# One transformer layer on one core: the second group's experts moved into the first pass, weighted values in bursts of a row, some weight splits on GpSimd

## The chip, the cores and the metric

The kernel runs on one core of a Trainium2 chip. The metric is the time of the device in microseconds. The kernel before took 824.49 us (median of 3 runs, 824.25 to 825.43); its profiled execution took 822.76 us, with a span of 821.0 us between the first and the last instruction.

## The reference, cut to what matters

The input x is 32 rows of 128 tokens of width 128. For all tokens:

```python
# 1. routed experts (8 of width 64, top 2) and a shared one of width 128
y = sum_over_experts(route_weight * (leaky(x @ w_gate) * (x @ w_up)) @ w_down)
y = y + (leaky(x @ sw_gate) * (x @ sw_up)) @ sw_down
# 2. banded attention of one head on y (span 32), layer norm, added to x
# 3. layer norm, then attention of 16 heads of width 64 with one shared key and value,
#    a null key, normed queries and keys, a position bias and a softmax over 129 keys
# 4. layer norm, then a feed-forward net 128 -> 2 x 512 (gated) -> 512 -> 512 -> 128,
#    added to the result of 2
```

All in float32. The kernel gets that precision for most projections from three matmuls with a weight and an input that are each split into a high part and a low part (`three`, L1199).

## The kernel before, in words

The 32 rows are worked on in 8 groups of 4 rows (512 tokens). A group goes through stage A (experts `rw`, `exp`, `down`; banded attention `qkv`, `scores`, `mix`; norms `ln1`, `ln2`; projections `xnT`, `kv`, `q`, and the sums `qs`, `qst`, `kT`), stage B (the attention of 16 heads: `sim`, `max`, `ex`, `inv`, `pn`, `PT`, `PV`, `z`) and stage C (feed-forward: `zT`, `l1` to `l4`). The stages are a software pipeline: a pass holds stage A of one group, stage B of the one before it and stage C of the one before that. The first pass ("fill") holds A of group 0 and the setting up, the second ("start") A of group 1 and B of group 0, then come five "steady" passes, "seventh", "last" and "drain".

Within a pass each engine follows a list written out by hand, `ORDER` (L53 to L192), one list for each engine and kind of pass; `passes` (L238) turns it into calls. Engines wait for each other by counting semaphores, and each engine is strictly in order: what waits blocks all behind it in its list. Step names in the lists have a number: `exp.0` to `exp.4` are five chunks of 128 hidden units (two groups of three matmuls, gate and up, and for `exp.0` to `exp.3` one matmul that spreads the routing weights), `sim.0` to `sim.11` three bursts of heads for each of four rows, `PT.0` to `PT.15` the transposes of four heads each, `PV.0` to `PV.7` the weighted values of eight heads each.

The PSUM banks come in rings: M of three, S of two (`sim`, `qs`), T of two (`PT`, `PV`). `bank_plan` (L251) gives banks in the order of TensorE's list, and `free` (L1205) makes TensorE wait until the last user of a bank has been drained. In the fill pass stage A uses a ring F of four banks (M and one of T).

What matters around the change:

- `experts_low` (`wl`, L828) and `part_low` (`pl`, L909) take the low parts of the weights on VectorE; `pl.0` to `pl.3` stand in the fill pass, `pl.4` and `pl.5` (h1 and h2, 2048 elements a partition each) in the start pass. Both h1 and h2 are loaded into `hA`, one after the other: `load_square` (`hw`, L515) waits for the split of h1 before it loads h2.
- The experts of a group: TensorE `expert` (L1225), ScalarE `expert` (L682) leaky gate out of PSUM, VectorE `expert` (L945) two products out of PSUM. `gs` and `hT` hold the results and are used again by stage A.
- SyncE's list: `load_x` (L519) loads the group's x in both layouts, after the table of the position bias has been written to memory and read back (L506 to L510). `flip_bias` (`fl`, L1192) on TensorE needs that read.
- GpSimd: `q_norm` (`qn`, L614) is a power of 16 columns for a row, `bias` (L619) adds the mask to the position bias for four heads, `p_norm` (`pn`, L631) multiplies four heads' exponentials by the inverse sums. `score` (`sim` on VectorE, L1078) waits for `qn` of its row, for `bias` of its heads and for the transposes that last read `sm`.
- `pv` on TensorE (L1332): for eight heads two matmuls, one into each half of the partitions, into one bank of T; ScalarE's `ot_copy` (L743) takes them out.
- `warm` (L1175) are matmuls whose results nobody reads; they stand in the fill pass alone.

## Time and profile before

| | us |
|---|---|
| median of 3 runs | 824.49 |
| profiled execution | 822.76 |
| its span | 821.0 |
| fill pass, to the first `sim.0` | 0 to 71.8 |
| start pass, to the next `sim.0` | 71.8 to 141.8 |
| a steady pass (five) | 94.7 to 95.1 |
| seventh, last, drain | 87.2, 94.1, 24.0 |

The passes are told apart by the matmuls of L1321 with number 0. Over the span TensorE has matmuls in flight for 786.9 us (96%), ScalarE is busy for 606.6 us, VectorE for 584.7 us and GpSimd for 448.9 us. A matmul's row shows how long it was in flight, and the next one starts before it ends, so starts are to be compared rather than durations. "Idle before" is the time that an engine stood still ahead of a row, and behind it stands what ended the wait.

### The profile page before, as it was taken

Reading aid. Unit: us, or ns where it says so; the run is one execution under the profiler, and the core shown is the slowest. Engines: PE = TensorE matmul, PEld = TensorE weight load, DVE = VectorE, ACT = ScalarE, POOL = GpSimd, SP = SyncE. Lnnn points to the kernel's source line nnn. Section 1 sums busy time; section 2 is a strip of 40 time slices with the busy share of each in tenths; the row PEclk is TensorE's granted clock in tenths of the full one; section 3 lists DMA queues with packets and bytes.
Section 4 is the critical chain, followed back from the end, with each engine's and each line's share of the span. In section 5 each row is a group of like instructions: output and inputs, shape, how many; then the busy total and the mean of one; then the engine's idle time right before and its main releaser. Section 6 shows DMA issues by size and latency. Waiting matters only on the chain.

```text
span 821.0 us, 16705 instructions
## 1 busy us (share of the span) xinstructions
PE 786.9 (96%) x5368; PEld 595.9 (73%) x5368; DVE 584.7 (71%) x1581; ACT 606.6 (74%) x1652; POOL 448.9 (55%) x388
## 2 busy tenths in 40 slices
...
DMA packets 15589, 16.99 MB, mean 21 GB/s; under 512 B 1408, under 2 KB 13072, under 8 KB 15120
## 3 DMA queue, kind: packets, MB, share of 16 engines
...
q10 hardware_dynamic: 304, 0.01, 0.0%
...
## 4 chain that ended last, share of the span: by engine, by line
PE 54%; ACT 19%; DVE 8%; issue 7%; POOL 5%; DVEq 0%; ACTq 0%; POOLq 0%
PE ps_M L1202 25%; ACT sb_sm L733 8%; PE ps_S L1321 5%; PE ps_z L1349 4%; PE ps_T L1336 4%; PE ps_T L1329 4%; PE ps_M L1248 4%; ACT L733 3%; PE ps_M L1381 3%; DVE sb_sm L1089 2%; ACT sb_al L774 2%; ACT L774 2%; PE ps_S L1303 2%; POOL sb_rq L617 2%; ACT sb_pT L740 2%
## 5 line engine op out<-in xcount | busy, mean ns | idle before, releaser
L733 ACT ACTIVATE sb_sm<-sb_sm,sb_nmx 128x129 f32<-128x129 f32 x512 | 199.2, 392 | 33.3 <-DVE sb_nmx L1097 32.8
L634 POOL TENSOR_TENSOR sb_sm<-sb_sm,sb_rden 128x512 f32<-128x512 f32 x128 | 135.8, 1064 | 144.9 <-DVE sb_rden L1102 144.9
L627 POOL TENSOR_TENSOR sb_biasm<-sb_bias,sb_maskn 128x512 f32<-128x512 f32 x128 | 170.9, 1343 | 79.0 <-DVE sb_sm L1089 55.0
L1089 DVE SCALAR_TENSOR_TENSOR sb_sm<-ps_S,sb_rq,sb_biasm 128x129 f32<-128x129 f32 x512 | 140.5, 342 | 55.9 <-PE ps_T L1329 43.2
L617 POOL TENSOR_TENSOR sb_rq<-sb_qss,sb_mhalf 128x16 f32<-128x16 f32 x32 | 92.1, 2903 | 27.4 <-DVE sb_qss L1074 27.4
L1321 PEld LDWEIGHTS ps_S<-sb_k,sb_qs 64*128 64x128 f32 x1024 | 65.1, 187 | 43.6 <-issue 43.1
L733 ACT ACTIVATION_READ_ACCUMULATOR sb_sm<-sb_sm,sb_nmx 128x1 f32 x512 | 96.6, 189 | 0.0
L740 ACT ACTIVATE sb_pT<-ps_T 128x512 f32<-128x512 f32 x128 | 74.4, 588 | 22.3 <-PE ps_T L1329 22.2
L1321 PE MATMUL ps_S<-sb_k,sb_qs 64*128 64x129 f32 x1024 | 83.0, 291 | 4.4 <-DVE sb_sm L1089 3.5
L1097 DVE TENSOR_REDUCE sb_nmx<-sb_sm 128x4 f32<-128x516 f32 x128 | 85.5, 675 | 0.4
L1329 PE MATMUL ps_T<-sb_ident,sb_sm 128*128 128x128 f32 x512 | 76.5, 276 | 3.6 <-POOL sb_sm L634 3.2
L1329 PEld LDWEIGHTS ps_T<-sb_ident,sb_sm 128*128 128x128 f32 x512 | 59.2, 141 | 17.1 <-issue 5.2
L1336 PE MATMUL ps_T<-sb_pT,sb_vs 128*64 128x512 f32 x256 | 66.4, 612 | 3.0 <-ACT sb_pT L740 3.0
L1349 PE MATMUL ps_z<-sb_wout,sb_oT 128*128 128x128 f32 x512 | 67.5, 279 | 0.4 <-ACT sb_oT L747 0.4
L1349 PEld LDWEIGHTS ps_z<-sb_wout,sb_oT 128*128 128x128 f32 x512 | 62.2, 192 | 5.2 <-ACT sb_oT L747 1.4
L1049 DVE TENSOR_SCALAR sb_qs<-ps_M,sb_cols 128x512 f32<-128x512 f32 x62 | 45.6, 744 | 16.9 <-ACT sb_gs L721 6.5
L1202 PE MATMUL ps_M<-sb_hBh,sb_h2h 128*128 128x512 f32 (+1 forms) x144 | 55.6, 386 | 0.8 <-DVE sb_hBl L923 0.8
L1202 PE MATMUL ps_M<-sb_hAh,sb_h1h 128*128 128x512 f32 (+1 forms) x144 | 55.0, 382 | 0.5 <-DVE sb_hAl L923 0.5
L1202 PE MATMUL ps_M<-sb_hAh,sb_h1l 128*128 128x512 f32 (+1 forms) x144 | 53.1, 369 | 0.0
L1202 PE MATMUL ps_M<-sb_hBl,sb_h2h 128*128 128x512 f32 (+1 forms) x144 | 53.1, 369 | 0.0
L1202 PE MATMUL ps_M<-sb_hBh,sb_h2l 128*128 128x512 f32 (+1 forms) x144 | 53.1, 369 | 0.0
L1202 PE MATMUL ps_M<-sb_hAl,sb_h1h 128*128 128x512 f32 (+1 forms) x144 | 53.1, 369 | 0.0
...
## 6 DMA issues: line engine op xcount, KB each, us to landing
...
sb_hA<-in_h SPq DMA_DIRECT2D x2, 1024.0 KB, 6.7
...
sb_sm<-toeplitz SPq DMA_DIRECT2D x1, 1024.0 KB, 5.8
...
```

Of the source, the lines that this page charges most:

```text
L617: pool.tensor_tensor(rq[:, cut], qss[:, cut], mhalf[:], ALU.pow).then_inc(q_rnorm.sem, 1)
L627: pool.tensor_tensor(biasm[:, heads, 1:NK], bias0[:, heads], maskn[:, j // 4].unsqueeze(1).broadcast_to([128, 4, S]), ALU.add)\
L634: pool.tensor_tensor(sm[:, heads, 1:NK], sm[:, heads, 1:NK], rden[:, heads].unsqueeze(2).broadcast_to([128, 4, S]), ALU.mult)\
L733: ins = act.activation(sm[:, h], sm[:, h], ACT.Exp, bias=nmx[:, h:h + 1], accum_out=den[:, h:h + 1])
L740: act.activation(pT[:, heads].rearrange("p h s -> p (h s)"), bank(g, "PT", j)[:], ACT.Copy)\
L1089: ins = dve.scalar_tensor_tensor(sm[:, h], bank(g, "sim", n, odd)[:, m * NK:(m + 1) * NK], rq[:, k * HEADS + h:k * HEADS + h + 1], biasm[: ...
L1097: dve.tensor_reduce(nmx[:, heads], sm[:, heads], AX, ALU.max, negate=True).then_inc(max_ready.sem, 1)
L1202: ins = pe.matmul(ps, w[i], x[j], start=start and n == 0, stop=stop and n == 2)
L1321: ins = pe.matmul(ps[odd][:, m * NK:(m + 1) * NK], qs[half, lo + m, k * S:(k + 1) * S], k2[half, k], start=True, stop=True)
L1329: ins = pe.transpose(ps[:, h * S:(h + 1) * S], sm[:, j % 4 * 4 + h, 1:NK], ident[:])
L1336: ins = pe.matmul(ps[DH * odd:DH * (odd + 1)].rearrange("p (h s) -> p h s", h=4), vs[:, n // 2], pT[:, n % 2 * 8 + odd:n % 2 * 8 + 8:2], s ...
L1349: ins = pe.matmul(zbank[:, k * D:(k + 1) * D], oT[:, c], wout[:, c], start=(c == 0), stop=(c == NP - 1))
```

## The change

- `pv` is called four times a group instead of eight; each call does the sixteen heads of a row in eight instructions, into both banks of T, and waits for all four `PT` copies of the row. ScalarE's copies stay eight.
- Stage N: `rwn`, `expn`, `xhn`, `xln` in the fill pass are `rw`, `exp`, `xh`, `xl` of group 1. Their steps are gone from the start pass. Group 1's gate tiles are in `x1`, its hidden tiles in `hA` and `res`; its x is loaded directly after the split of group 0's, ahead of the position table. The load of h1 (`hw.0`) moves to the start pass, behind group 1's `down`; h2's stays behind h1's split.
- `wl` and `pl.0` to `pl.3` are done by GpSimd, `wl` in two instructions of 640 columns; `pl.4` and `pl.5` stay on VectorE.
- All lists are written anew.

```diff
     "pe fill": """
-        lg.0 warm.0 pb.0 warm.1-5 pb.1 warm.6 lg.1-2 warm.7 rw.0 exp.0 lg.3-4 exp.1 lg.5 exp.2 lg.6 pb.2 lg.7
-        exp.3 warm.8 exp.4 down.0 warm.9 pb.3 warm.10 qkv.0 scores.0 mix.0 warm.11-13 fl.0-2 warm.14 fl.3 xnT.0
-        warm.15-16 q.0-2 kv.0 q.3 qs.0-2 q.4-7 qs.3-7 warm.17 qst.0 kT.0 warm.18-21
+        lg.0 warm.0 pb.0 warm.1-4 pb.1 warm.5 lg.1-2 warm.6-7 lg.3 rw.0 exp.0 lg.4 pb.2 lg.5 exp.1 lg.6-7 exp.2
+        warm.8 pb.3 warm.9 exp.3-4 down.0 warm.10 fl.0 warm.11 qkv.0 scores.0 warm.12 rwn.0 mix.0 expn.0 fl.1
+        warm.13-16 expn.1 warm.17 fl.2-3 expn.2 xnT.0 expn.3 q.0-1 kv.0 q.2-4 qs.0-3 q.5-7 qs.4-7 qst.0 warm.18
+        expn.4 warm.19-20 kT.0 warm.21
     "pe start": """
-        sim.0 rw.0 sim.1 exp.0-1 sim.2 exp.2 sim.3 exp.3 PT.0-1 exp.4 PV.0 sim.4 PT.2 down.0 PT.3 sim.5 PT.4
...
+        sim.0-1 down.0 sim.2 PT.0-1 sim.3 PT.2 sim.4 qkv.0 PT.3 scores.0 sim.5 PV.0 mix.0 PT.4-5 sim.6-7 z.0
...
     "act start": """
...
+        ex.0-2 down.0 PT.0 ex.3 PT.1-2 qkv.0 ex.4 PT.3 ex.5 PV.0-1 ex.6-7 ph.4 PT.4-7 ex.8 PV.2 ex.9-10 PV.3
+        PT.8 xnT.0 ex.11 PT.9-10 q.0 ex.12 PT.11 ph.5 ex.13 PV.4 q.1 PV.5 q.2-3 ex.14 q.4 ex.15 PT.12-13 q.5-7
     "dve fill": """
...
+        xl.0 cg.0 rt.0 pb.0 nk.0 pb.1 rt.1-4 pb.2 x0.0 rw.0 pb.3 nk.1 exp.0-1 rt.5-6 exp.2-3 rt.7 exp.4 rt.8
+        down.0 xln.0 rt.9 qkv.0 rwn.0 scores.0 maskn.0 mix.0 expn.0 ln1.0 expn.1 ln2.0 expn.2 xnT.0 expn.3 q.0-1
+        kv.0 q.2-4 kT.0 q.5 ssq.0 ssc.0 expn.4 q.6 vs.0 q.7
     "dve start": """
...
+        sim.0 max.0 sim.1 max.1 inv.0-1 max.2 sim.2 inv.2 max.3 sim.3 down.0 sim.4 inv.3 max.4-5 qkv.0 inv.4
+        scores.0 inv.5 sim.5 max.6-7 mix.0 inv.6 sim.6 inv.7 ln1.0 max.8 sim.7 max.9 ln2.0 inv.8 max.10 sim.8
+        inv.9 pl.4 inv.10 max.11 xnT.0 sim.9 inv.11 max.12 sim.10 maskn.0 max.13 q.0 sim.11 kv.0 inv.12-13 q.1
+        max.14-15 q.2-3 inv.14 kT.0 q.4 inv.15 q.5-6 ssq.0 pl.5 ssc.0 q.7 vs.0
     "pool fill": """
-        pb.0-1 nb.0 nk.0 xb.0 ln1.0 ln2.0 bias+.0-2 kv.0 bias+.3 qn.0-3
+        pb.0 nb.0 wl.0 pb.1 xb.0 pl.0 nk.0 ln1.0 ln2.0 pl.1-2 bias+.0-2 kv.0 bias+.3 pl.3 qn.0-3
     "pool start": """
...
+        bias.4 pn.0-1 bias.5 pn.2 bias.6-8 pn.3 bias.9 xb.0 pn.4-5 bias.10-11 ln1.0 bias.12 pn.6-7 ln2.0 pn.8-9
     "sp start": """
-        rw.0 hw.1 maskn.0
+        own.0 hw.0 maskn.0 hw.1
...
-            def pv(g, n):
+            def pv(g, k):
-                ps = free(g, "PV", n, 0, (v_shifted, 1), (pt_copied, 2 * n + 2))
-                for odd in range(2):
...
+                for n in (2 * k, 2 * k + 1):
+                    ps = free(g, "PV", k, n % 2, (v_shifted, 1), (pt_copied, 4 * k + 4))
+                    for odd in range(2):
...
+            def experts_low(g, k):
+                pool.wait_ge(w_high, 1)
+                for n in range(2):
+                    pool.tensor_tensor(wgu[1][:, n], wgu_raw[:, n], wgu[0][:, n].bitcast(fp32), ALU.subtract).then_inc(w_low, 1)
+
+            def part_low(g, k):
+                name = PARTS[k]
+                pool.wait_ge(parts_high[name], 1)
+                pool.tensor_tensor(parts[name][1][:], raw[name], parts[name][0][:].bitcast(fp32), ALU.subtract)\
+                    .then_inc(parts_low[name], 1)
...
             def load_square(g, k):
-                sp.wait_ge(*((routed, 2 * ROUTE_OPS), (parts_low["h1"], 1))[k])
+                sp.wait_ge(*((y_psum.sem, y_psum.at(1, 1)), (parts_low["h1"], 1))[k])
```

In the steady list of TensorE the twelve `sim` bursts, the chunks and the layers are the same steps as before in another order; `PV` stands in four places there (five runs of `PV` before), and the runs of 512 column matmuls of L1202 are 20 instead of 16. In the seventh list `PV` has 4 runs instead of 8, in the last and the start list 4 instead of 7.

## Rows read from the trace of the kernel before

**Rows 1.** Windows by pass: busy us (instructions) of PE, PEld, DVE, ACT, POOL; clock, DMA.
```profile
0.00:71.80 71.80, 56.63 (x361) 44.48 (x361) 50.16 (x145) 24.46 (x41) 20.56 (x45) 0.98 0.37 129
71.80:141.80 70.00, 63.98 (x484) 45.10 (x483) 61.56 (x163) 53.05 (x174) 54.56 (x41) 1.00 0.08 26
331.60:426.30 94.70, 93.90 (x638) 70.71 (x637) 69.11 (x186) 73.29 (x201) 54.06 (x45) 1.00 0.05 10
615.70:702.90 87.20, 86.19 (x587) 62.54 (x587) 65.80 (x181) 70.74 (x198) 56.69 (x46) 1.00 0.01 1
702.90:797.00 94.10, 91.16 (x623) 72.74 (x620) 54.47 (x154) 80.38 (x212) 45.49 (x38) 1.00 0.02 7
```

**Rows 2.** Windows, two stretches of the start pass, same columns.
```profile
69.97:87.00 17.03, 15.52 (x109) 11.83 (x110) 15.38 (x40) 12.26 (x36) 17.03 (x10) 1.00 0.00 1
87.00:141.80 54.80, 50.28 (x393) 34.98 (x393) 48.01 (x127) 41.99 (x141) 39.36 (x32) 1.00 0.10 33
```

**Rows 3.** Timeline, head of the start pass: start, us, engine, what.
```profile
69.97 8.64 POOL L617 TENSOR_TENSOR sb_rq<-sb_qss,sb_mhalf 128x16 f32<-128x16 f32 x3 [2.50 <-DVE sb_qss L1074]
...
82.68 2.04 POOL L634 TENSOR_TENSOR sb_sm<-sb_sm,sb_rden 128x512 f32<-128x512 f32 x2
...
86.11 1.64 DVE L1089 SCALAR_TENSOR_TENSOR sb_sm<-ps_S,sb_rq,sb_biasm 128x129 f32<-128x129 f32 x6
```

**Rows 4.** Lines of the expert step: count, ns minimum/median/maximum, first and last start.
```profile
L687 ACT ACTIVATE sb_gs<-ps_M x39: 572/597/602, 21.9 to 627.4; 128x512 f32<-128x512 f32 x39
L958 DVE TENSOR_TENSOR sb_hT<-ps_M,sb_gs x31: 690/692/694, 26.8 to 626.5; 128x512 f32<-128x512 f32 x31
```

**Rows 5.** Timeline, expert matmuls of a steady pass.
```profile
332.44 0.50 PE L1202 MATMUL ps_M<-sb_xh,sb_wguh 128*128 128x512 f32 x1
332.78 0.39 PE L1202 MATMUL ps_M<-sb_xl,sb_wguh 128*128 128x512 f32 x1
333.01 0.40 PE L1202 MATMUL ps_M<-sb_xh,sb_wgul 128*128 128x512 f32 x1
```

**Rows 6.** Timeline, fill pass: splits, position table, first qkv.
```profile
12.23 1.49 DVE L830 TENSOR_TENSOR sb_wgul<-sb_hT,sb_wguh 128x1280 fp32r<-128x1280 f32 x1
...
40.72 0.47 PE L1202 MATMUL ps_M<-sb_yTh,sb_wqkvh 128*128 128x512 f32 x1 [0.66 <-issue]
...
42.97 0.34 ACT L670 ACTIVATE sb_pT<-ps_S,sb_pb 16x128 f32<-16x128 f32 x1
...
50.68 4.34 PE L1196 MATMUL ps_S<-sb_sm,sb_pT 128*128 128x512 f32 x6 [2.80 <-DMA sb_sm<-toeplitz]
...
59.32 1.22 DVE L912 TENSOR_TENSOR sb_w12l<-sb_al,sb_w12h 128x1024 fp32r<-128x1024 f32 x1
```

**Rows 7.** Timeline, a GpSimd addition, then VectorE and GpSimd side by side.
```profile
95.46 1.29 POOL L607 TENSOR_TENSOR sb_xs<-sb_xs,sb_rows 128x512 f32<-128x512 f32 x1
...
108.15 1.61 DVE L1017 TENSOR_TENSOR sb_hT<-sb_hT,sb_rows 128x512 f32<-128x512 f32 x1
...
132.71 2.65 DVE L912 TENSOR_TENSOR sb_h2l<-sb_hA,sb_h2h 128x2048 fp32r<-128x2048 f32 x1
...
133.16 3.10 POOL L634 TENSOR_TENSOR sb_sm<-sb_sm,sb_rden 128x512 f32<-128x512 f32 x1
...
136.31 0.66 PE L1329 MATMUL ps_T<-sb_ident,sb_sm 128*128 128x128 f32 x4 [2.00 <-POOL sb_sm L634]
```

**Rows 8.** The page's DMA issues, loads of h1 and h2.
```profile
sb_hA<-in_h SPq DMA_DIRECT2D x2, 1024.0 KB, 6.7
```

**Rows 9.** Timeline, PV in a steady pass: two calls in a row, and one alone.
```profile
360.28 1.94 PE L1336 MATMUL ps_T<-sb_pT,sb_vs 128*64 128x512 f32 x8
...
362.27 0.72 PE L1321 MATMUL ps_S<-sb_k,sb_qs 64*128 64x129 f32 x8
...
386.84 1.08 PE L1336 MATMUL ps_T<-sb_pT,sb_vs 128*64 128x512 f32 x4 [0.61 <-ACT sb_pT L740]
387.85 0.94 PE L1321 MATMUL ps_S<-sb_k,sb_qs 64*128 64x129 f32 x12
```

More of the change, by code:

```diff
@@ L67 @@
[L67 to L69 removed]
+        sim.0 rw.0 exp.0-1 sim.1 exp.2-3 sim.2 exp.4 down.0 sim.3 zT.0 PT.0-1 qkv.0 l1.0-1 PT.2 l1.2 scores.0
+        PT.3 l1.3 sim.4 PV.0 sim.5 l2.0 PT.4 l2.1 z.0 sim.6 PT.5 l2.2 z.1 l2.3 PT.6 mix.0 PT.7 sim.7 l3.0 sim.8
@@ L118 @@
-        exp.4 rt.8 down.0 rt.9 qkv.0 scores.0 mix.0 pl.1 ln1.0 pl.2 ln2.0 xnT.0 maskn.0 pl.3 q.0-2 kv.0 q.3-5
-        kT.0 ssq.0 ssc.0 q.6-7 xl.0 vs.0
+        xl.0 cg.0 rt.0 pb.0 nk.0 pb.1 rt.1-4 pb.2 x0.0 rw.0 pb.3 nk.1 exp.0-1 rt.5-6 exp.2-3 rt.7 exp.4 rt.8
+        down.0 xln.0 rt.9 qkv.0 rwn.0 scores.0 maskn.0 mix.0 expn.0 ln1.0 expn.1 ln2.0 expn.2 xnT.0 expn.3 q.0-1
+        kv.0 q.2-4 kT.0 q.5 ssq.0 ssc.0 expn.4 q.6 vs.0 q.7
     """,
     "dve start": """
-        xl.0 rw.0 sim.0 max.0 sim.1 exp.0 max.1 exp.1 sim.2 inv.0 max.2 inv.1 exp.2 max.3 inv.2 exp.3 sim.3
@@ L123 @@
-        inv.3 max.4 sim.4 inv.4 max.5 exp.4 max.6 inv.5 down.0 sim.5 inv.6 max.7 pl.4 qkv.0 scores.0 sim.6 inv.7
-        max.8 mix.0 sim.7 inv.8 max.9 ln1.0 sim.8 inv.9 max.10-11 ln2.0 inv.10 sim.9 xnT.0 max.12 inv.11 sim.10
-        inv.12 max.13-14 q.0 kv.0 sim.11 q.1 maskn.0 inv.13 q.2-3 max.15 q.4 inv.14 kT.0 inv.15 q.5 pl.5 ssq.0
-        q.6 ssc.0 q.7 vs.0
+        sim.0 max.0 sim.1 max.1 inv.0-1 max.2 sim.2 inv.2 max.3 sim.3 down.0 sim.4 inv.3 max.4-5 qkv.0 inv.4
+        scores.0 inv.5 sim.5 max.6-7 mix.0 inv.6 sim.6 inv.7 ln1.0 max.8 sim.7 max.9 ln2.0 inv.8 max.10 sim.8
@@ L132 @@
-        max.11 ln2.0 inv.9-11 sim.9 xnT.0 max.12 kv.0 maskn.0 sim.10 q.0 inv.12 max.13 q.1 max.14 q.2 inv.13
-        sim.11 l4.0 max.15 inv.14 kT.0 q.3-5 inv.15 ssq.0 q.6 ssc.0 q.7 vs.0
+        xl.0 rw.0 ln3.0 sim.0 exp.0-1 sim.1 exp.2 max.0 exp.3 max.1 inv.0 exp.4 max.2 sim.2 zT.0 max.3 inv.1-2
+        down.0 zl.0 sim.3 max.4 inv.3 qkv.0 l1.0-1 h1.0-1 l1.2-3 sim.4 scores.0 max.5 h1.2 inv.4 h1.3 max.6
+        sim.5 max.7 inv.5-6 h2.0 inv.7 sim.6 max.8 h2.1-2 mix.0 h2.3 sim.7 max.9 inv.8 sim.8 max.10-11 inv.9
@@ L134 @@
+        ln1.0 ln2.0 inv.10-11 xnT.0 sim.9 kv.0 sim.10 max.12 inv.12 max.13-14 q.0 inv.13 kT.0 q.1 inv.14 l4.0
+        q.2 sim.11 max.15 maskn.0 q.3 inv.15 q.4 ssq.0 q.5-6 ssc.0 vs.0 q.7
     """,
     "dve seventh": """
-        rw.0 xl.0 ln3.0 exp.0 sim.0 exp.1-2 sim.1 max.0 exp.3-4 inv.0 max.1-2 zT.0 inv.1 sim.2 max.3 down.0
-        inv.2 zl.0 inv.3 sim.3 qkv.0 l1.0-1 h1.0 max.4 l1.2 h1.1 sim.4 h1.2 max.5 l1.3 max.6 scores.0 h1.3 inv.4
-        sim.5 inv.5 max.7 inv.6 sim.6 inv.7 max.8 mix.0 sim.7 inv.8 max.9-10 ln1.0 sim.8 max.11 inv.9 h2.0 ln2.0
```

179 lines of the change are left out of this document (95 added, 84 removed).

## The prediction

> **What bounds the kernel now.** I read the windows by pass first. In a steady pass TensorE has work in flight for 93.9 of 94.7 us while VectorE has 69 and ScalarE 73 [rows 1]: there, and in the seventh pass, the order of TensorE's own list is the time, and other engines count only where they make it stand. In the start pass it is otherwise: TensorE 64, VectorE 61.6, GpSimd 54.6 of 70.0 us, and in the fill pass nobody is full (56.6 and 50.2 of 71.8), which is a chain of latencies. So the work that the change takes out of the start pass is worth what that pass's own bounds allow, and I read those in two stretches.
>
> Head of the start pass: from 69.97 us, when the inverse norms of group 0 begin, to 87.0 us GpSimd is busy 17.03 of 17.03 us [rows 2]. It does four powers of 2.9 us (three of them are the 8.64 us row), one bias, two normalisations (2.04 us) and a bias, and then VectorE can start the fourth burst of scores at 86.11 us [rows 3]: 86.11 - 69.97 = 16.1 us that GpSimd sets alone. Rest of the start pass: 54.8 us with VectorE busy 48.0 and TensorE 50.3 [rows 2]: VectorE with its waits.
>
> **The change part by part.** My clock is the profiled execution (822.76 us, 1.7 us below the median of the runs); I take differences from it and put them on the median, 824.5.
>
> *Experts of group 1, out of the start pass.* Removed from it: on TensorE 4 x 7 + 6 = 34 matmuls of 0.23 us (332.78 to 333.01 us [rows 5]), 7.9 us; on VectorE 9 products of 0.69 us [rows 4], 6.2 us, and the split of x, 0.7; on ScalarE 5 gates of 0.6 us [rows 4] and two copies, 4.2 us. Almost all of VectorE's part (exp.0 to exp.3, eight products) stands before 86.11 us, that is inside the 16.1 us of GpSimd, whose list at that point is the same steps as before. There it buys nothing unless VectorE then does later work early, and the new list of VectorE has down.0 only behind sim.3. So of 6.2 us I count only exp.4, 0.6 us (results start 0.6 us apart), and on TensorE the four routing transposes, 0.5 us, now behind the next sim.0. The bounds are 0 and TensorE's 7.9 us.
>
> *VectorE's split of h2 (pl.5).* It now stands between ssq and ssc, beside TensorE's PV.3 of 2 us. Before, it ran at 132.71 us beside the last normalisation, which took 3.10 us against a usual 1.04, and TensorE stood 2.00 us for it [rows 7]. I count -2.2 us with the restart. What is late next: h2's load can only be issued behind pl.4, which has moved from the row of the fifth maximum to behind inv.9; the load takes 6.7 us [rows 8], and ph.5 stands in ScalarE's list four ScalarE steps of about 6 us later, with the exponentials ex.13 and all of group 1's remaining squares queued behind it. I price that wait at +0.9 us (0 to 4).
>
> *Start pass, smaller things.* PV in 4 runs and not 7 (below), -0.4 us; four entries fewer into 512 column runs at 0.1 us (0.34 against 0.23 us to the next start [rows 5]), -0.4. Sum of the start pass: -0.6 - 0.5 - 2.2 + 0.9 - 0.8 = -3.2 us (-10 to +2).
>
> *Fill pass.* Added on its way: 34 expert matmuls, 9 products and 5 gates, 0.7 us of split, and the routing transposes. Taken off VectorE: wl 1.49 us, and the splits pl.0 to pl.3, of which w12 has 1.22 us for 1024 columns [rows 6]. The new products stand one pair (1.3 us) in each place where VectorE waited for a power on GpSimd or for a transpose, and the 8 us of matmuls where TensorE did warming up; VectorE has 71.8 - 50.2 = 21.6 us free there [rows 1]. So most of it is hidden. What isn't, by my walk through the lists: TensorE does lg.3 and an extra warm ahead of exp.0 (about +0.8 us on its start at 20.7); fl.0 and a warm stand ahead of qkv.0, which began at 40.72 us. fl.0 needs the position table, which landed 7.7 us behind the copy at 42.97 us [rows 6]. In the new lists that copy stands before exp.3, at about 33 us by my walk, so the table is there at about 41, just when the low part of y is. The rest of the chain keeps its lengths. On GpSimd the splits cost, by the nearest row, an addition of two tiles, 1.29 us for 512 columns [rows 7]: wl 3.2 us, wq2 and w12 2.6 us each; the other end is VectorE's price, half of that. wl can start when its high part is there (about 16 us) and ends at 19, before TensorE is at exp.0; wq2 ends about 1 us before q.0 wants it; w12 lies between the last bias of row 0 and the first power, where GpSimd waited 2.50 us [rows 3]. If that cover were gone they would cost 2.6 us at most at the last place. I take +1.5 us for the fill pass (-1 to +5).
>
> A rule bears on this. Where GpSimd and VectorE both work on tiles in SBUF the rows show stretched instructions: an addition of VectorE took 1.61 us beside GpSimd, and one of GpSimd 3.10 us beside VectorE's split [rows 7]. The Trainium skill, SBUF — State Buffer, section "Who interferes with whom", says that a VectorE instruction with two SBUF inputs and a GpSimd instruction that reads SBUF exclude each other for the whole instruction, whichever comes first. By that rule each split on GpSimd (3 us for wl) can stop VectorE's routing chain of small two-input steps for its own length, up to some 3 us at the start of the fill pass; by the rows the stretch is the other's remaining time, which is the same thing, and TensorE's logits cover it here. It goes into the upper end for the fill pass alone.
>
> *PV in one burst.* Two calls in a row took 362.27 - 360.28 = 1.99 us, one alone 387.85 - 386.84 = 1.01 us and about 0.1 of entry [rows 9]: a merge gives 0.1 to 0.15 us, no more. One steady run of PV stood 0.61 us for ScalarE's copy of the transposes between two calls [rows 9]; in the new list a layer and two bursts of scores stand in that place, so it goes. Steady pass: -0.6 - 0.14, and four more entries into 512 column runs at up to 0.1 us, +0.25: -0.5 us, five times, -2.5 us (a pass -2 to +1.2, since the order is new and its stalls can't be read from the old trace). Seventh: four merges, -0.5; last: three, -0.4 and -0.3 for its waits, ScalarE having 80 of 94 us [rows 1]: -1.2 us together. The drain list is the same but for two swaps: 0.
>
> Sum: -3.2 + 1.5 - 2.5 - 1.2 = -5.4 us; 824.5 - 5.4 = 819.1, told as 819 us.
>
> **The rivals.**
> *The moved experts are worth their full TensorE time.* The start pass would shrink by 7.9 us and the fill pass hide all: 824.5 - 7.9 - 0.5 (start's other gains less the wait for h2) - 3.2 = 813 us. For it: TensorE's 7.9 us and VectorE's 6.2 lie in the passes where VectorE has 61.6 of 70 us [rows 1]. Against it: GpSimd's 17.03 of 17.03 us at the head [rows 2].
> *The fill pass gets longer.* One mechanism: fl.0 stands in front of qkv.0, so if the position table lands later than y's low part all of stage A of group 0 waits for it. Each microsecond of lateness is one of the total. The total turns slower when the table lands more than 5.4 us later than I reckon, at 46.5 us; it landed at 50.6 before [rows 6]. If the copy ahead of it came at 42 us again and not at 33: +8.5 us, 827.5 us. Against it: ScalarE's new list has that copy in front of two expert chunks.
> *What one pass gives the next takes.* The fill pass takes +4, the start pass gives -3.2, the steady order gives nothing: 824.3 us, no change. For it: the steady passes have few stalls to give.
> That merged PV does not do what it says is not a rival of its own; it is worth under 2 us in all.
>
> **How the numbers follow.** Forecast 0.47 (its own range 815 to 823), full worth 0.27, no change 0.12, longer fill (or another new stall of this size) 0.14. What can be told from no change is 0.2%, 1.6 us. Of the forecast's case 0.02 falls inside the 0.2%, and the no-change case spills a little to both sides: faster 0.73, same 0.12, slower 0.15. Range: the full-worth case gives the low end with the steady passes at -1 us each, 811; the high end takes in no change and the beginning of the longer fill, 826.
>
> **What would show it.** The first sim.0 at 73.3 us (71.8 before); the first power of GpSimd 1.5 us later and the fourth score burst again 16.1 us behind it; start to steady at about 140 us instead of 141.8; ph.5 with a wait for a DMA; steady passes of 94.2 us; no wait of PV for L740 in them. Wrong if: the score burst comes sooner than 16 us behind the first power, or a new wait of over 1 us appears in every steady pass.

## The result, and the profile after

The changed kernel takes 829.50 us (median of 8 runs, 826.82 to 834.75) against 824.37 us of the kernel before in the same session (8 runs, 822.18 to 826.25): ratio 1.0071, 95% interval 1.0056 to 1.0085. It is slower by about 5.9 us; 819 us was forecast (811 to 826), faster. The profiled execution took 826.82 us, the shortest of the eight, its span 824.9 us; that of before has a span of 821.0 us, so the two traces differ by 3.9 us, and the table below accounts for these 3.9.

I cut both traces where TensorE turns the sums of the query squares of the next group (before: 69.4, 139.3, ... 613.3, 700.2 us). Windows of the changed kernel by pass (fill, start, third steady, seventh), then the start pass of the kernel before between the same two cuts; columns as in [rows 1]:

```profile
0.00:75.10 75.10, 60.59 (x370) 48.45 (x370) 59.23 (x145) 26.80 (x45) 26.16 (x50) 0.98 0.31 109
75.10:144.50 69.40, 59.01 (x452) 42.32 (x453) 52.76 (x150) 50.26 (x168) 55.46 (x41) 0.95 0.13 41
334.90:429.70 94.80, 93.80 (x637) 70.89 (x635) 67.81 (x185) 72.72 (x201) 54.67 (x44) 1.00 0.04 10
619.30:703.60 84.30, 83.38 (x574) 62.42 (x572) 67.35 (x183) 69.75 (x197) 54.93 (x44) 1.00 0.00 1
```
```profile
69.40:139.30 69.90, 63.88 (x485) 45.06 (x483) 61.60 (x160) 53.05 (x174) 54.59 (x40) 1.00 0.08 26
```

| stretch | before | after | difference | forecast |
|---|---|---|---|---|
| fill pass | 69.4 | 75.1 | +5.7 | +1.5 |
| start pass | 70.0 | 69.4 | -0.6 | -3.2 |
| five steady passes | 474.0 | 474.8 | +0.8 | -2.5 |
| seventh | 86.9 | 84.3 | -2.6 | with the next: -1.2 |
| last and drain | 120.8 | 121.3 | +0.5 | |

The forecast cut the passes elsewhere, at the first `sim.0`, so its column doesn't fit these rows exactly. By its own cut the changed kernel has the first `sim.0` at 80.4 us (71.8 before, 73.3 forecast) and the next one at 146.5 us (141.8 before, about 140 forecast):

```profile
80.43 0.94 PE L1351 MATMUL ps_S<-sb_k,sb_qs 64*128 64x129 f32 x12 [0.49 <-ACT sb_k L756]
```

By that cut the fill pass grew by 8.6 us where +1.5 was forecast, and the start pass shrank by 3.9 us where -3.2 was forecast. The two cuts differ because the first score burst comes 5.3 us behind the turned sums and no longer 2.4: the last expert quarter and the turn of the keys stand between them. GpSimd's powers, and with them the head of the start pass, begin at the turned sums in both kernels, so I keep that cut. By it the start pass lost 5 us of TensorE's busy time and 9 of VectorE's (TensorE's last moved quarter is still inside it), yet it is as long as it was, and the fill pass grew by four times what I had given it. The timeline of the changed kernel there (start, us, engine, what; columns as in [rows 6]), and behind it the norm in the kernel before:

```profile
55.29 0.46 POOL L612 TENSOR_TENSOR sb_wkv2l<-sb_res,sb_wkv2h 128x128 fp32r<-128x128 f32 x1
55.36 5.24 DVE L1031 TENSOR_SCALAR sb_hT<-sb_x,sb_mv,sb_rstd 128x128 f32<-128x128 f32 x4
...
55.70 2.37 POOL L612 TENSOR_TENSOR sb_wq2l<-sb_oT,sb_wq2h 128x1024 fp32r<-128x1024 f32 x1
...
58.04 3.71 POOL L655 TENSOR_TENSOR sb_biasm<-sb_bias,sb_maskn 128x512 f32<-128x512 f32 x3
...
60.66 0.65 PE L1308 MATMUL ps_T<-sb_ident,sb_hT 128*128 128x128 f32 x3 [3.69 <-DVE sb_hT L1031]
```
```profile
55.73 1.11 DVE L1002 TENSOR_SCALAR sb_hT<-sb_x,sb_mv,sb_rstd 128x128 f32<-128x128 f32 x4 [1.19 <-POOL sb_rstd L599]
```

The row to read is VectorE's second layer norm of group 0: four instructions, 5.24 us. In the kernel before the same four took 1.11 us, with GpSimd idle. Here GpSimd runs two low parts and three bias products at the same time, its own rows at their usual length, and TensorE stands 3.69 us for the norm. Behind that wait its clock is low; the timeline of TensorE just after, and the window around it:

```profile
61.74 0.63 PE L1232 MATMUL ps_M<-sb_xl,sb_wguh 128*128 128x512 f32 x1
62.17 0.63 PE L1232 MATMUL ps_M<-sb_xh,sb_wgul 128*128 128x512 f32 x1
```
```profile
61.00:64.50 3.50, 3.50 (x11) 2.83 (x10) 1.97 (x4) 1.28 (x2) 0.75 (x1) 0.52 0.00 0
84.00:90.30 6.30, 6.30 (x14) 2.41 (x11) 3.18 (x10) 4.29 (x22) 6.30 (x5) 0.73 0.00 0
```

Matmuls of 512 columns start 0.43 us apart, where they are 0.23 apart in [rows 5]: granted clock 0.52, the lower of the two levels (1.2 GHz) for all of it. The second window is the down product of the start pass, behind 2 us of TensorE's waiting. A second collision stands at the end of the fill (changed kernel, then the norm of the keys before):

```profile
71.12 3.07 DVE L1091 TENSOR_TENSOR sb_hT<-sb_hT,sb_rk 128x256 f32<-128x256 f32 x2
...
71.34 2.57 POOL L612 TENSOR_TENSOR sb_w12l<-sb_al,sb_w12h 128x1024 fp32r<-128x1024 f32 x1
...
75.11 0.33 PE L1340 MATMUL ps_S<-sb_ident,sb_ssT 128*128 128x128 f32 x1 [1.34 <-DVE sb_ssT L1098]
```
```profile
67.26 0.83 DVE L1061 TENSOR_TENSOR sb_hT<-sb_hT,sb_rk 128x256 f32<-128x256 f32 x2
```

The norm of the keys took 0.83 us before and takes 3.07, beside the low part of w12. The query copy and the sums stand behind it on VectorE. Adding up: 4.1 us of the first collision, 1.4 of the slow clock behind it (seven matmuls 0.20 us later each) and 2.2 of the second are 7.7; the pass grew by 5.7, so some of it was hidden. What was hidden can be told from the stretch that holds both collisions, from the first matmul of qkv to the turned sums: 28.6 us before (40.72 to 69.36), 34.0 in the changed kernel (41.09 to 75.11).

### The profile page after: what moved, and what is told of

The parts are those of the page before. It is cut to its first block, busy times and chain, and to the rows that moved or that the text cites. A ratio compares the mean times of both kernels' runs of the same rounds, so it can differ in the third digit from the quotient of the medians.

```text
span 824.9 us, 16692 instructions
## 1 busy us (share of the span) xinstructions
PE 786.3 (95%) x5368; PEld 601.0 (73%) x5368; DVE 579.7 (70%) x1576; ACT 601.5 (73%) x1650; POOL 459.5 (56%) x394
## 4 chain that ended last, share of the span: by engine, by line
PE 72%; DVE 10%; POOL 6%; issue 5%; ACT 5%; DMA 0%; DVEq 0%; ACTq 0%; POOLq 0%
PE ps_M L1232 38%; PE ps_S L1351 7%; PE ps_T L1359 5%; PE ps_z L1380 5%; PE ps_T L1367 5%; PE ps_M L1278 3%; DVE sb_sm L1119 3%; POOL sb_rq L645 3%; ACT sb_sm L762 2%; POOL sb_biasm L655 2%; POOL sb_sm L662 2%; PE ps_S L1333 2%; DVE sb_hT L1031 1%; PE ps_M L1302 1%; PE ps_M L1308 1%
## 5 line engine op out<-in xcount | busy, mean ns | idle before, releaser
L662 POOL TENSOR_TENSOR sb_sm<-sb_sm,sb_rden 128x512 f32<-128x512 f32 x128 | 139.8, 1095 | 212.7 <-DVE sb_rden L1132 212.7
L762 ACT ACTIVATE sb_sm<-sb_sm,sb_nmx 128x129 f32<-128x129 f32 x512 | 199.0, 393 | 29.7 <-DVE sb_nmx L1127 29.2
L655 POOL TENSOR_TENSOR sb_biasm<-sb_bias,sb_maskn 128x512 f32<-128x512 f32 x128 | 165.7, 1309 | 0.6 <-DVE sb_sm L1119 0.6
L1380 PEld LDWEIGHTS ps_z<-sb_wout,sb_oT 128*128 128x128 f32 x512 | 64.1, 194 | 5.2 <-ACT sb_oT L776 1.9
L1367 PE MATMUL ps_T<-sb_pT,sb_vs 128*64 128x512 f32 x256 | 62.0, 605 | 0.0
L947 DVE TENSOR_TENSOR sb_hBl<-sb_al,sb_hBh 128x512 fp32r<-128x512 f32 (+1 forms) x36 | 30.6, 861 | 41.0 <-ACT sb_hBh L809 41.0
L1232 PE MATMUL ps_M<-sb_hAl,sb_h1h 128*128 128x512 f32 (+1 forms) x144 | 53.2, 369 | 0.0
L1232 PE MATMUL ps_M<-sb_hAh,sb_h1l 128*128 128x512 f32 (+1 forms) x144 | 53.2, 369 | 0.0
```

The source lines that it names most:

```text
L655: pool.tensor_tensor(biasm[:, heads, 1:NK], bias0[:, heads], maskn[:, j // 4].unsqueeze(1).broadcast_to([128, 4, S]), ALU.add)\
L662: pool.tensor_tensor(sm[:, heads, 1:NK], sm[:, heads, 1:NK], rden[:, heads].unsqueeze(2).broadcast_to([128, 4, S]), ALU.mult)\
L762: ins = act.activation(sm[:, h], sm[:, h], ACT.Exp, bias=nmx[:, h:h + 1], accum_out=den[:, h:h + 1])
L1232: ins = pe.matmul(ps, w[i], x[j], start=start and n == 0, stop=stop and n == 2)
L1367: ins = pe.matmul(ps[DH * odd:DH * (odd + 1)].rearrange("p (h s) -> p h s", h=4), vs[:, k], pT[:, n % 2 * 8 + odd:n % 2 * 8 + 8:2], start= ...
L1380: ins = pe.matmul(zbank[:, k * D:(k + 1) * D], oT[:, c], wout[:, c], start=(c == 0), stop=(c == NP - 1))
```

## The experiments

Each was timed in five rounds beside the kernel before on the same chip (its medians 823.6 to 824.7 us). The first four settle the fill pass. Theory A: GpSimd's work beside VectorE's norms did it. Rival B: the experts moved into the pass did it. Rival C: the bursts or the new order did it.

**GpSimd waits for the norm** (a1_wait_norm). The changed kernel with, in GpSimd's low part of wkv2 (all GpSimd's later work of the fill stands behind it), two lines more:

```
+                if k == 1:
+                    pool.wait_ge(n2_ready.sem, n2_ready.at(0, 1))
```

> The changed kernel with one wait more: GpSimd begins its second, third and fourth low part (one after the other, pl.1 first) only when VectorE has finished the second layer norm of group 0. The changed kernel stands at 829.5 us (1.0071 of the kernel before). Theory A (GpSimd's low parts and bias products held up the layer norm of group 0, 5.24 us where it took 1.11, and the norm of the keys, 3.07 where it took 0.83, and TensorE's clock fell behind the first of them): the layer norm is back near 1.1 us, TensorE's 3.69 us wait for it is gone and the score matmuls of the fill begin some 4 us earlier; the bias products come about 6 us later, so part of it may be lost at their end; 824 to 826 us. Rival B (the fill is longer because VectorE and TensorE have four more expert quarters in it): nothing moves, 828.5 to 830 us. Rival C (the burst of weighted values or the written-out order costs it in the later passes): nothing moves either.

826.91 us, ratio 1.003 (1.001 to 1.005): 3.4 us better than the changed kernel, 0.9 short of what A expected. The norm is back, and TensorE's wait now is a short one for the low part (timeline):

```profile
60.23 1.12 DVE L1033 TENSOR_SCALAR sb_hT<-sb_x,sb_mv,sb_rstd 128x128 f32<-128x128 f32 x4
...
61.85 2.40 POOL L614 TENSOR_TENSOR sb_wq2l<-sb_oT,sb_wq2h 128x1024 fp32r<-128x1024 f32 x1
...
64.30 0.51 PE L1234 MATMUL ps_T<-sb_yTh,sb_wq2h 128*128 128x512 f32 x1 [0.42 <-POOL sb_wq2l L614]
```

The fill pass of this trace still ends at 75.2 us, as in the changed kernel, but for another reason. Its execution (830.16 us) is one of the long ones of its twelve. The first qkv starts at 45.97 us, 4.9 us late, in steps ahead of the edit: TensorE's first expert matmuls of 512 columns start 0.43 us apart and not 0.23, and its routing matmuls run as slowly from about 17 us on, although the clock column of the profile has 1.00 there (timeline):

```profile
25.65 0.63 PE L1234 MATMUL ps_M<-sb_xl,sb_wguh 128*128 128x512 f32 x1
26.08 0.63 PE L1234 MATMUL ps_M<-sb_xh,sb_wgul 128*128 128x512 f32 x1
```

From there to the turned sums it takes 29.2 us, against 34.0 in the changed kernel. So taking GpSimd's work away from beside the norm wins 4.8 us of the 5.4. The norm of the keys still takes 3.08 us here, so the second collision is nearly all hidden: 0.6 us at most are left for it.

**The low parts back on VectorE** (b1_splits_dve)**; then the mask late as well** (b2_splits_dve_mask_late). The second edit is on top of the first, which gives wl and pl back to VectorE's lists, with one difference from the kernel before: `pl.3`, the low part of w12, stands in the start pass. The fill of both, and of the later kernels that are built on the second, is spared its 1.2 us of VectorE. The second edit, written on the lines of the first:

```
-        ... scores.0 maskn.0 mix.0 pl.1 expn.0 ln1.0 pl.2 expn.1 ln2.0 expn.2 xnT.0 expn.3 ...
+        ... scores.0 mix.0 pl.1 expn.0 ln1.0 pl.2 expn.1 ln2.0 maskn.0 expn.2 xnT.0 expn.3 ...
```

> The changed kernel with the low parts of the first weights back on VectorE (wl and pl.0 to pl.3 at the places that the kernel before gives them beside the same neighbours, pl.1 to pl.3 2.1 us in all); the bias products of GpSimd stay where the change has them. Theory A: half of the cause is gone. The two low parts no longer run beside the layer norm and none beside the norm of the keys, but the three bias products (3.71 us for three, begun at the mask) still run beside the layer norm: the norm takes 2.5 to 4 us instead of 5.24, the norm of the keys 0.8 instead of 3.07; 825.5 to 828 us. Rival B: 829.5 to 832 us, since VectorE gets 2 us or more of work back.

> As b1_splits_dve, and the mask of group 0 is written behind the second layer norm, so that GpSimd's bias products, which wait for it, start behind that norm. Theory A: nothing of GpSimd is left beside the layer norm: it takes about 1.1 us, the fill comes back to within 1.5 us of the kernel before, and the gain of the seventh pass (2.6 us) stays; 822 to 825 us. Rival B: as b1_splits_dve within 0.5 us, 829.5 to 832 us.

Measured 828.10 us, 1.0058 (1.0034 to 1.0083), and 825.75 us, 1.0016 (1.0000 to 1.0033). With the bias products alone beside it (timeline, first kernel) the norm takes their length:

```profile
54.93 3.73 POOL L655 TENSOR_TENSOR sb_biasm<-sb_bias,sb_maskn 128x512 f32<-128x512 f32 x3
55.12 3.87 DVE L1036 TENSOR_SCALAR sb_hT<-sb_x,sb_mv,sb_rstd 128x128 f32<-128x128 f32 x4
```

and with nothing beside it (second kernel) 1.11 us again:

```profile
57.58 1.11 DVE L1036 TENSOR_SCALAR sb_hT<-sb_x,sb_mv,sb_rstd 128x128 f32<-128x128 f32 x4
...
59.10 3.79 POOL L655 TENSOR_TENSOR sb_biasm<-sb_bias,sb_maskn 128x512 f32<-128x512 f32 x3 [1.68 <-DVE sb_maskn L1090]
```

**The low parts alone, on the kernel before** (c1_before_splits_pool). wl and pl.0 to pl.3 go from VectorE's fill list to GpSimd's (shown), with the waits that this needs; nothing else:

```
-        pb.0-1 nb.0 nk.0 xb.0 ln1.0 ln2.0 bias+.0-2 kv.0 bias+.3 qn.0-3
+        pb.0 nb.0 wl.0 pb.1 xb.0 pl.0 nk.0 ln1.0 ln2.0 pl.1-2 bias+.0-2 kv.0 bias+.3 pl.3 qn.0-3
```

> The kernel before with one part of the change alone: the low parts of the first weights (wl, pl.0 to pl.3) on GpSimd, at the places of its list that the change gives them; experts, weighted values and every other order as before. Its bias products wait for the mask, which VectorE writes behind the layer norm. Theory A: the two low parts ahead of the bias products (0.46 and 2.37 us) run as soon as their high parts are there, beside whatever VectorE does then, so a norm or a statistics chain is held by up to 2.4 us, and the last one (2.57 us) beside the norm of the keys or the query statistics; VectorE is relieved of about 3 us ahead of it; 824 to 828 us. Rival B (moving the splits to an idle engine is a gain in the fill, the loss is the experts'): 821.5 to 823.5 us.

827.02 us, 1.0027 (1.0013 to 1.0041): slower than before although VectorE has less to do and no expert was moved. Its timeline:

```profile
57.07 3.28 DVE L1008 TENSOR_SCALAR sb_hT<-sb_x,sb_mv,sb_rstd 128x128 f32<-128x128 f32 x4 [1.41 <-POOL sb_rstd L610]
...
57.41 2.35 POOL L595 TENSOR_TENSOR sb_wq2l<-sb_oT,sb_wq2h 128x1024 fp32r<-128x1024 f32 x1
```

Its fill pass ends at 73.7 us, 4.3 later than before, and only half of that lies at the norms. The other half comes first: wl on GpSimd stands beside VectorE's work for the position table (0.34 and 0.29 us for the same two instructions in the kernel before), TensorE waits 5.29 us for that and no longer 2.81, and the first qkv starts 2.2 us later (timeline):

```profile
11.55 1.61 DVE L856 TENSOR_SCALAR sb_pT<-sb_pT,sb_pmv,sb_prs 128x128 f32<-128x128 f32 x1 [0.19 <-POOL sb_prs L578]
11.55 3.02 POOL L590 TENSOR_TENSOR sb_wgul<-sb_hT,sb_wguh 128x640 fp32r<-128x640 f32 x2
13.20 1.53 DVE L857 TENSOR_TENSOR sb_pT<-sb_pT,sb_rows 128x128 f32<-128x128 f32 x1
15.21 0.45 PE L1191 MATMUL ps_S<-sb_ident,sb_pT 128*128 128x128 f32 x1 [5.29 <-ACT sb_pT L674]
```

So the norm behaves as A says in all four, though the times of a1, b1 and b2 lie 0.9, 0.1 and 0.8 us above A's ranges: with 0, 2.8, 3.7 and 6.5 us of GpSimd beside them the same four instructions took 1.11, 3.28, 3.87 and 5.24 us. The stretch from the first qkv to the turned sums follows:

| kernel | GpSimd beside the norm, us | first qkv to turned sums, us |
|---|---|---|
| before | 0 | 28.6 |
| c1 | 2.8 | 30.8 |
| b1 | 3.7 | 32.7 |
| changed, e1 | 6.5 | 34.0 each |
| a1 | 0 | 29.2 |
| b2, f1, g1, h1, n1 | 0 | 28.8 each |

(The kernels from e1 on are told below.) B falls for this stretch: the last six kernels have four of the five moved expert chunks in it (the expectations call them quarters) and are within 0.6 us of the kernel before. Up to the turned sums the fill passes of f1, g1, h1 and n1 take 69.2, 68.4, 68.8 and 69.0 us, no more than before, so these four need not cost the fill anything. The fifth chunk stands behind the turned sums, and there the first `sim.0` comes later: at 74.5 us in f1, 71.8 before. Two others end at 71.1 (b2) and 74.4 us (f2, whose stretch takes 31.9); there TensorE's clock was 0.63 from 20 to 24 us (b2) and 0.66 from 60 to 70 us (f2).

**The later passes by themselves.** First (w1_before_head_new_tail) the fill and start pass of the kernel before, with the change's orders behind them and bursts of two rows everywhere; then (w2_before_head_single) the same with single rows in the start pass:

```
+                if g == 0:
+                    ps = free(g, "PV", k, 0, (v_shifted, 1), (pt_copied, 2 * k + 2))
...
+                    return
```

> The kernel before in its fill pass and start pass (experts, low parts and order as they were), but with the weighted values in bursts of two rows everywhere, and the change's written-out orders of the steady passes, the seventh, the last and the drain. It holds only what the change did to the later passes. By the two profiles the steady passes are equal (95.0 against 94.9 us a pass), the seventh is 2.6 us shorter in the changed kernel and the last with the drain 0.5 longer: 822 to 823 us, 0.9975 of the kernel before. Rival C (the bursts or the new order cost the time): 826 us or more. Rival F (the seventh pass is only shorter because it makes up for a state it inherits from a later start): 824 to 825 us.

> As w1_before_head_new_tail (830.35 us, its start pass 79.7 us where the kernel before has 70.0, its seventh 84.3 where that has 86.9), but in the start pass the weighted values stay one row at a time, in the order of the kernel before: nothing at all is changed up to the end of the start pass; the bursts of two rows and the new orders begin with the first steady pass. Theory I (the bursts cost nothing in the steady passes and the seventh gains 2.6 us; in the start pass a burst that waits for four turns of the probabilities holds TensorE's queue): the start pass is back at 70.0, the last pass with the drain takes 121.8 as in w1; 821.3 to 822.8 us against 823.6 to 824.5 of the kernel before, ratio 0.996 to 0.999. Rival F (the later passes gain only what an earlier pass lost): ratio 1.000 or more.

The first took 830.35 us, 1.0075 (1.0059 to 1.0092), all of its loss in the start pass: 79.7 us. I had to choose the places of the bursts there, and one of them stops three queues (timeline):

```profile
97.13 3.53 PE L1337 MATMUL ps_T<-sb_pT,sb_vs 128*64 128x512 f32 x8 [2.36 <-ACT sb_pT L740]
98.99 0.69 ACT L747 ACTIVATE sb_oT<-ps_T,sb_cols 128x512 f32<-128x512 f32 x1 [2.01 <-PE ps_T L1337]
101.49 0.61 DVE L1089 SCALAR_TENSOR_TENSOR sb_sm<-ps_S,sb_rq,sb_biasm 128x129 f32<-128x129 f32 x2 [5.80 <-PE ps_S L1321]
```

The second took 822.18 us, 0.9975 (0.9963 to 0.9988): **faster than both kernels**. Its steady passes are 94.8 us, its seventh 84.3, the last with the drain 121.7. Rival F (the seventh is only shorter because of a later start) falls, and C falls for these passes: the change's later passes are a gain of about 2 us, which comes from the seventh. What the bursts cost in the start pass of the changed kernel is not told by this.

**Is the start pass bound by GpSimd?** (e1_after_short_powers) Group 0's powers on 4 of 16 columns; the other twelve are only copied:

```
+                    pool.tensor_tensor(rq[:, cut], qss[:, cut], mhalf[:, 0:4], ALU.pow).then_inc(q_rnorm.sem, 1)
```

> The changed kernel (829.5 us) with less GpSimd work at the head of the start pass: for group 0 it raises only 4 of the 16 columns of each row's query norms to the power and copies the other 12, so twelve of sixteen powers of that group are left out. The four powers take 11.76 us at the head of that pass; they should take 3 to 4. Theory G (the head of the start pass is bound by GpSimd, so that taking the experts away from it gave only 0.5 us): the start pass gets 5 to 8 us shorter and the time falls to 822 to 824.5 us. Rival H (VectorE or the order binds it): 828 to 830 us.

829.87 us, 1.0071 (1.0052 to 1.0089): nothing. A power takes 1.01 us and its copy 0.1, so the four take 4.4 us and not 11.8. The fourth score burst (the row at 93.23 of this kernel's timeline) starts 15.9 us behind the first power; it was 16.1 in [rows 3] and 17.7 in the changed kernel (75.78 to 93.49):

```profile
77.36 1.01 POOL L648 TENSOR_TENSOR sb_rq<-sb_qss,sb_mhalf 128x4 f32<-128x4 f32 x1
...
93.23 1.65 DVE L1124 SCALAR_TENSOR_TENSOR sb_sm<-ps_S,sb_rq,sb_biasm 128x129 f32<-128x129 f32 x6 [0.16 <-PE ps_S L1356]
```

With 7.4 us less on GpSimd the burst came 1.8 us sooner, and the pass took 70.0 us against 69.4. Even these 1.8 us are not GpSimd's: from the start of the down product to the third score burst, which stands behind it on TensorE, it is 4.5 us here at full clock (85.58 to 90.07) and 6.2 in the changed kernel at the lower one (84.14 to 90.33). G falls for the changed kernel, and with it the bound on which my forecast of the head rested. The rows say what waits instead: VectorE's first burst stood for a power in the kernel before (0.67 us) and stands for TensorE's scores in the changed kernel:

```profile
81.48 1.65 DVE L1119 SCALAR_TENSOR_TENSOR sb_sm<-ps_S,sb_rq,sb_biasm 128x129 f32<-128x129 f32 x6 [1.77 <-PE ps_S L1351]
```

**Is it TensorE's clock?** Idle matmuls ahead of four waits of the start pass, in b2 (f1_start_warm); and, in another, two expert quarters back there (f2_two_quarters_back, `sim.0 exp.3 sim.1 exp.4 down.0`):

```
+            def warm_start(g, k):
+                for n in range(4):
+                    pe.matmul(zbank[:, 3 * D:4 * D], ident[:], ident[:], start=True, stop=True)
...
-        sim.0-1 down.0 sim.2 PT.0-1 sim.3 PT.2 sim.4 qkv.0 ...
+        sim.0 ws.0-2 sim.1 down.0 sim.2 PT.0-1 sim.3 PT.2 ws.3-5 sim.4 qkv.0 ...
```

> The kernel of b2_splits_dve_mask_late (825.75 us, 1.0016) with eleven idle units more on TensorE in the start pass: each is four 128x128 matmuls of the identity into a corner of a bank that nobody reads, three units ahead of each of the score bursts 1, 4 and 7 of group 0 and two ahead of the eleventh turn of the probabilities, the places where its profile shows TensorE waiting 1.90, 2.08, 1.92 and 1.57 us and then matmuls of 512 columns spaced 0.43 us where they are spaced 0.23 elsewhere. Theory D (with the experts gone TensorE stands idle in the start pass, its granted clock falls behind each such wait, and the work behind it, down, qkv, the queries, comes late): the granted clock of the start pass goes from about 0.87 to 1.0 and the pass gets 2 to 4 us shorter; 822 to 824 us. Rival E (the pass is bound by GpSimd and VectorE, TensorE's clock costs nothing there): the clock rises and the time stays at 825 to 826.5 us, or gets up to 1 us worse for the added 6.6 us of TensorE.

> The kernel of b2_splits_dve_mask_late (825.75 us, 1.0016) with the last two quarters of group 1's experts (exp.3 and exp.4) back in the start pass, between the first score bursts, and three left in the fill. Theory D: the fill gets about 1.5 us shorter (two quarters fewer beside the query projections), and in the start pass TensorE has 2.5 us of work where it waited, so the clock stays up longer; 822.5 to 824.5 us. Rival E (the start pass is bound by VectorE, which gets 3 us of products back at its head): the fill gains 1.5 and the start pass loses 1.5 to 3, 825.5 to 827.5 us.

824.75 us, 1.0008 (0.9993 to 1.0023), and 828.52 us, 1.0042 (1.0023 to 1.0061). The windows of the start pass, without and with the idle matmuls:

```profile
71.10:145.80 74.70, 63.07 (x451) 46.90 (x451) 55.15 (x151) 50.14 (x168) 55.92 (x41) 0.89 0.12 38
```
```profile
69.20:139.70 70.50, 65.89 (x539) 50.53 (x539) 55.01 (x151) 50.07 (x168) 55.73 (x41) 1.00 0.12 40
```

The clock went from 0.89 to 1.00 and the pass of that trace is 4.2 us shorter, but the first trace is of one of the longest executions of its kernel (829.38 us, median 825.75). The ratios, 1.0016 and 1.0008, differ by 0.7 us and their intervals overlap. D (the clock costs the pass 2 to 4 us) is not shown beyond that. The quarters put back made it slower than E (the clock costs nothing there) expected, but this kernel's runs lie in two heaps: four at 824.0 to 824.8 us with a mean clock of 0.993 or 0.994, and seven of the other eight at 828.1 to 831.4 with 0.986 to 0.988. The first heap is what D expected, the second is not, and its trace has the slow stretch at 60 to 70 us named above. So it decides nothing on the start pass.

**Is it the written order?** Three rewrites of f1: the keys ahead of the last quarter (h1_keys_first, `kT.0 expn.4` for `expn.4 ... kT.0`), group 1's chain earlier (g1_chain_earlier, the lines below and the like on the other engines), and single rows of weighted values (n1_start_single):

```
-        ... PT.0-1 sim.3 PT.2 ws.3-5 sim.4 qkv.0 PT.3 scores.0 sim.5 PV.0 mix.0 ...
+        ... PT.0-1 qkv.0 sim.3 PT.2 scores.0 ws.3-4 sim.4 mix.0 PT.3 sim.5 PV.0 ...
```

> The kernel of f1_start_warm (824.75 us, 1.0008), with the turn of the keys ahead of the last expert quarter on TensorE and ScalarE, and the last quarter's products behind the query copies on VectorE; the change has it the other way round. In the profile of f1_start_warm the first score burst of the start pass comes 5.3 us behind the turned sums of the queries, in the kernel before 2.4 us. Theory L (the experts in the fill cost 2.9 us at the head of the start pass, and group 0's softmax starts that much later): the first burst comes 2.5 to 3 us earlier and half or more of that reaches the end, 821.5 to 823.5 us. Rival M (the head is made up by the fourth burst, since GpSimd's powers and biases hold it there): the first burst is earlier, the fifth is not, 824 to 825.5 us.

> The kernel of f1_start_warm (824.75 us, 1.0008), with the start pass written in another order: group 1's down product, its split, qkv, scores and mix come one to two score bursts earlier on TensorE, ScalarE, VectorE and GpSimd. In the profile of f1_start_warm the down product was ready at 83.7 us, ScalarE copied it at 85.78 behind two more bursts of exponentials, VectorE split it at 89.76 behind its fourth score burst, and qkv began at 91.4; none of the four engines was busy for more than nine tenths of that stretch. Theory J (the start pass did not get shorter without its experts because the written order still keeps group 1's chain behind group 0's softmax, not because an engine is full): qkv begins 3 to 5 us earlier and the pass gets 2 to 5 us shorter, 820 to 823 us. Rival K (VectorE and GpSimd bound the pass, the chain only swaps places with the softmax): qkv is earlier, the last score bursts later, 824 to 826 us.

> The kernel of f1_start_warm (824.75 us, 1.0008; start pass 70.5 us) with the weighted values of group 0 one row at a time in the start pass (each a pair of turns earlier than the second half of its burst, with its copy on ScalarE likewise); bursts of two rows from the first steady pass on, experts in the fill, everything else as there. In the order of the kernel before, bursts in the start pass cost 8 us (w1_before_head_new_tail against w2_before_head_single). Theory N (the start pass did not get shorter without its experts because the burst, which waits for four turns, holds TensorE's and ScalarE's queues): the start pass falls from 70.5 to 64 to 67 us, 819 to 822 us. Rival O (the bursts of the change's own start list stand where they hold nobody; 8 us was the price of their place in the other list): 824 to 825.5 us.

825.53 us, 1.0021 (1.0011 to 1.0032); 828.47 us, 1.0050 (1.0034 to 1.0066); 838.42 us, 1.0182 (1.0157 to 1.0207). The start passes are 73.7, 78.1 and 86.3 us against 70.5. In the second, qkv does begin 5.9 us earlier (85.47 us against 91.40), and the pass is 7.6 us longer; in the third one misplaced call holds TensorE alone for over 5 us:

```profile
109.64 1.98 PE L1377 MATMUL ps_T<-sb_pT,sb_vs 128*64 128x512 f32 x4 [5.15 <-ACT sb_pT L771]
```

In the first M was nearest: the first `sim.0` came 1.9 us earlier (72.65 us against 74.53) and the time did not fall. In the others neither J nor K, neither N nor O came out. What they show is how steep the order is: it moved this pass by 3 to 16 us, while in the window of f1 above the fullest engine has 65.9 us of 70.5. Whether an order exists in which the freed time is won stays open.

**The best version with warm waits** (w3_tail_and_warm). The kernel of 822.18 us, with idle matmuls at two waits that the kernel before has too (`mix.0 warm.11-13 warm.22-29 fl.0-2`, `kT.0 ws.0-2 PT.15`):

> The kernel of w2_before_head_single (822.18 us, 0.9975) with idle matmuls for TensorE at two places where it waits in the kernel before as well: eight units of two ahead of the flips of the position bias in the fill (it waits 2.81 us there for a load, and the flips behind it then take 4.1 us at a granted clock of 0.73 to 0.66 where they take 1.9 at full clock), and three units of four ahead of the last turn of the probabilities of the start pass (2.00 us of waiting). Theory D (the clock falls behind waits of some 2 us and what follows is on the path): the clock of these stretches stays at 1.0, 820 to 821.5 us, 0.995 to 0.997 of the kernel before. Rival E (what follows is hidden): 822 to 823 us, with the mean clock at 1.000.

822.46 us, 0.9981 (0.9971 to 0.9992): the clock is 1.000 in nine of twelve runs and the ratio is the same within the intervals. Rival E holds here. The best version stays the one without.

## Why the prediction was wrong

*Fill pass.* The failed step is the sentence that set the exclusion aside: "TensorE's logits cover it here. It goes into the upper end for the fill pass alone." What failed is a cost that the term of +1.5 us put at nothing. I weighed the rule for wl beside the routing chain. There it was harmless in the changed kernel (the routing weights came 0.8 us later; in c1, where wl started earlier, it met the position table and cost 2.2 us). I did not walk the other low parts and the bias products, which the change also moves forward by putting the mask ahead of mix, past the two norms of the chain. What the runs show in its place: the layer norm takes 5.24 us and not 1.11, TensorE stands 3.69 us for it, and the stretch around it is 34.0 us long and not 28.6; with the collision taken away it is 28.8 to 29.2. The Trainium skill, SBUF — State Buffer, section "Who interferes with whom", names both kinds: a VectorE instruction in a 2-port mode, which tensor_scalar can enter, excludes a GpSimd instruction, and one with two SBUF inputs a GpSimd instruction that reads SBUF; whichever is first has the ports for its whole length. The trace agrees: 3.87 us of norm beside 3.73 of GpSimd, 3.07 beside 2.57. No row names the mode that the norm ran in. The step "w12 lies between the last bias of row 0 and the first power, where GpSimd waited" saw GpSimd's free time and not whom it would block. The priced rival of this sign (position table late) did not happen: the first qkv began at 41.09 us, 0.4 later than in [rows 6]. GpSimd's own prices were right: wl 3.03 us (3.2 reckoned), wq2 2.37 (2.6).

By the forecast's own cut at the first `sim.0` there is a second miss of 2.9 us in this pass (80.4 us against 73.3 forecast): the first burst stands behind the last moved quarter and the keys. Taking 1.9 of it away (h1) did not shorten the kernel.

*Start pass.* "16.1 us that GpSimd sets alone" was a reading of busy time as a bound. GpSimd was busy 17.03 of 17.03 us in [rows 2], but with 7.4 us of that taken away the burst moved by 1.8 only. By the forecast's own cut this pass is 3.9 us shorter (-3.2 forecast), but 2.9 of that is only its start pushed into the fill; by mine it is 0.6. That the experts bought little at the head came true, for a wrong reason: that it fits is luck. In the changed kernel's trace the head, from the turned sums to the fourth score burst, grew from 16.8 to 18.4 us (-1.1 forecast), and the rest of the pass shrank from 53.2 to 51.0 (-2.1 forecast). In e1, whose list is the same, they are 16.7 and 53.4, so this split is only sure to some 2 us. The stall of [rows 7] did go: TensorE's last transposes wait for no normalisation, and of the last four normalisations two take their usual 1.02 us each, the others 1.47 and 1.04. The split of h2 now lengthens the bias products instead, three in 5.86 us where three take 3.7 (timeline of the changed kernel):

```profile
133.69 2.04 POOL L662 TENSOR_TENSOR sb_sm<-sb_sm,sb_rden 128x512 f32<-128x512 f32 x2 [6.52 <-DVE sb_rden L1132]
...
139.92 5.86 POOL L655 TENSOR_TENSOR sb_biasm<-sb_bias,sb_maskn 128x512 f32<-128x512 f32 x3
...
142.37 2.28 DVE L936 TENSOR_TENSOR sb_h2l<-sb_hA,sb_h2h 128x2048 fp32r<-128x2048 f32 x1
```

What the -2.2 us for it were worth no run tells by itself. The wait for h2's load, priced at 0.9 us, did not come: ScalarE's copy of h2 at 128.39 us has no wait ahead of it.

*Steady passes.* The wait of [rows 9] went, as forecast: TensorE's row of it is gone in the third steady pass, with 0.6 us of waiting for query copies in its place, and the pass is 94.8 us, not 94.2. The first steady pass grew 0.8. Term of -2.5: measured +0.8. Removing one wait of 0.6 us did not shorten the pass.

*Seventh and last.* -1.2 forecast, -2.1 measured: near as a sum and the largest gain, but not by the forecast's terms. The seventh was given -0.5 for its merged PV and measured -2.6, the last -0.7 and measured +0.5. w2 has the same two (84.3, and 121.7 against 120.8), so the gain of the seventh is real; which part of its new list gives it no run tells. A slip of the prediction's sums belongs here too: the full-worth rival is given 813 us with 0.5 and 3.2 us for the other gains, where the prediction's own terms are 2.1 and 3.7, which would make 810.8.

All together: from the changed kernel (1.0071) to the best version (0.9975) are 7.9 us, the 5.9 of loss and the 2.0 that the later passes gain. The low parts and the early bias products are 4.5 of them (1.0071 to 1.0016). The other 3.4 lie in the new head, fill and start pass, without the collision: some 0.7 us may be TensorE's clock (1.0016 to 1.0008), and 2.7 us go with the rest of the new head, its order, its experts and its bursts together, and are open.
